# Where the products in front of a cross-attention are issued: into the tail of the mixture's blocks, on two fixed sets of banks

## The reference, cut to what matters

```python
x = x + _L0_xattn_ref(_layernorm(x), ctx_512, ctx_512)
x = x + _L0_ffn_ref(_layernorm(x), ...)        # 2 of 8 experts per token, then the weighted sum of two rows
x = x + _L1_xattn_ref(_layernorm(x), ctx_512, Wq, w_kc_q, w_kc_kv, W_qr, W_kr, Wo)   # 16 heads
x = x + _L1_ffn_ref(_layernorm(x), ...)        # 1 of 32 masked experts per token

q_hk  = (hidden_q @ Wq.T).reshape(Bv, Sv, H, K)
q_big = jnp.einsum('bshk,hkq->bshq', q_hk, w_kc_q)          # Wq and w_kc_q can be multiplied beforehand
q_r   = jnp.einsum('bshq,hqr->bhsr', rope(q_big), W_qr)
k_r   = jnp.einsum('bld,hdr->bhlr', kv_r, W_kr)
scores = jnp.einsum('bhsr,bhlr->bhsl', q_r, k_r)            # W_qr and W_kr likewise
ctx_lat = jnp.einsum('bhsd,hkd->bhsk', ctx_c, w_kc_kv)
return ctx @ Wo.T                                           # w_kc_kv and Wo likewise
```

## Time and profile before

| | us |
|---|---|
| median of 3 runs (range) | 478.03 (476.23 to 480.19) |
| profiled execution, its own time | 480.91 |
| its span, first to last instruction | 479.0 |
| busy in the span: PE / DVE / ACT / POOL | 379.1 / 347.0 / 213.7 / 137.9 |
| mean granted clock of TensorE | 0.919 of full speed |

### The profile page before, as it was taken

One profiled execution on the slowest core, in us unless ns is written; L12 is line 12 of the kernel. 1 busy time (PEld: TensorE's weight loads), 2 busy tenths in 40 slices (PEclk: granted clock), 3 DMA queues, 4 the chain that ended last, 5 costly groups with the idle time before them and its releaser, 6 DMA issues.

```text
span 479.0 us, 10598 instructions
## 1 busy us (share of the span) xinstructions
PE 379.1 (79%) x3676; PEld 259.6 (54%) x3677; DVE 347.0 (72%) x876; ACT 213.7 (45%) x474; POOL 137.9 (29%) x147
## 2 busy tenths in 40 slices
PE   2566867771687778797989999999999989548991
PEld 1344545671244444575555664664655878436881
DVE  4998898979788989386686876977868525663551
ACT  1578787825278778479010231221211321224440
POOL 1064000020667774300031421412403410161332
PEclk9989798955589999899999999999999999859997
DMA  8975562041144661171021120220220201341010
GB/s 299 423 300 189 191 219 104 10 168 46 39 132 152 196 200 57 46 263 36 1 90 47 42 90 9 82 89 2 89 89 1 89 1 54 124 130 58 25 35 22
DMA packets 16895, 50.77 MB, mean 106 GB/s; under 512 B 2072, under 2 KB 6304, under 8 KB 14800
## 3 DMA queue, kind: packets, MB, share of 16 engines
q1 hardware_dynamic: 13984, 42.46, 24.6%
q0 software_dynamic: 2864, 7.68, 5.3%
HBM read 43.44 MB, written 6.69 MB: 105 GB/s over the span
## 4 chain that ended last, share of the span: by engine, by line
PE 61%; DVE 14%; ACT 10%; issue 8%; POOL 5%; DMA 1%; ACTq 0%; DVEq 0%; POOLq 0%
PE bank L941 15%; PE bank L1147 7%; PE bank L953 6%; PE bank L1024 6%; PE bank L964 3%; PE bank L837 3%; PE bank L650 2%; PE bank L1000 2%; PE bank L977 2%; DVE mx L1426 2%; PE bank L803 2%; POOL y_rows L589 2%; ACT pnat L1166 2%; ACT W L1180 2%; POOL xg L582 1%
## 5 line engine op out<-in xcount | busy, mean ns | idle before, releaser
L1637 DVE TENSOR_TENSOR roped<-bank,cst 128x512 f32<-128x512 f32 x96 | 61.8, 686 | 30.2 <-PE bank L941 28.6
L596 POOL TENSOR_TENSOR WE<-WE,wT 128x512 f32<-128x512 f32 x32 | 40.5, 1299 | 140.9 <-DMA WE<-_L_ffn_expert_masks_dram 140.9
L1307 ACT ACTIVATE qrT<-bank 128x512 f32<-128x512 f32 x16 | 8.7, 596 | 82.2 <-PE bank L964 82.2
L941 PE MATMUL bank<-XNT_hi,AW_hi 128*128 128x512 f32 x96 | 41.3, 430 | 2.3 <-DVE roped L1637 1.6
L941 PE MATMUL bank<-XNT_hi,AW_lo 128*128 128x512 f32 x96 | 37.8, 394 | 0.0
L941 PE MATMUL bank<-XNT_lo,AW_hi 128*128 128x512 f32 x96 | 37.8, 393 | 0.0
L953 PE MATMUL bank<-roped,MW 128*64 128x512 f32 x128 | 31.0, 605 | 0.0
L1024 PE MATMUL bank<-VW,ctxT 128*128 128x256 f32 x128 | 30.8, 386 | 0.0
L941 PEld LDWEIGHTS bank<-XNT_hi,AW_hi 128*128 128x128 f32 x96 | 18.0, 187 | 22.0 <-DVE roped L1637 12.1
L582 POOL DMA_INDIRECT xg<-x_rows,owner_b x23 | 22.8, 993 | 24.0 <-DVE owner_b L420 14.8
L803 PE MATMUL bank<-W,xgT 128*128 x92 | 27.1, 422 | 2.2 <-ACT xgT L1243 2.2
(11 more groups left out here) (297 smaller groups left out, 893.9 us busy)
## 6 DMA issues: line engine op xcount, KB each, us to landing
raw<-in_L_ffn_w_dram SPq DMA_DIRECT2D x8, 1536.0 KB, 6.4
fold<-in_L_xattn_fold_dram SPq DMA_DIRECT2D x8, 1024.0 KB, 5.2
WE<-_L_ffn_expert_masks_dram SPq DMA_DIRECT2D x8, 1024.0 KB, 5.4
kv<-in_keys_values_dram SPq DMA_DIRECT2D x8, 656.0 KB, 7.6
yg<-y_rows SPq DMA_DIRECT2D x8, 256.0 KB, 4.7
x_tok<-pay SPq DMA_DIRECT2D x8, 256.0 KB, 2.3
X<-in_x_dram SPq DMA_DIRECT2D x4, 256.0 KB, 9.3
ctx_sb<-in_ctx_dram SPq DMA_DIRECT2D x1, 768.0 KB, 18.4
```

What stands on the lines that cost most here:

```text
L596: pool.tensor_tensor(WE[:, e], WE[:, e], wT[:], ALU.mult).then_inc(WE_ready, 1)
L941: mm = pe.matmul(bank[g][:], a[:, k, c * P:(c + 1) * P], b[:, k, g * 512:(g + 1) * 512], start=k == 0 and i == 0, stop=k == 1 and i == 2)
L1637: ins = dve.tensor_tensor(roped[n][:, r, :].rearrange("p (b s) -> p b s", s=S), src, cst[:, None, at:at + S].to_broadcast([P, 8, S]), ALU. ...
```

## The change

The fold of unit 0 is finished inside the tail: its query halves are issued one before and one after the turn of block 20, its values behind them, its keys after the turn of block 21; unit 1's query halves stand around the turn of block 22. ACT copies unit 0's rounded halves out between `hidT` and `y` of the last two blocks. Even units use banks 7, 0, 1, 3 and odd units 2, 4, 5, 6. Units 0, 1 and 2 (before: 0 and 1) are split by DVE straight from the bank. The variances are taken in two halves of four tiles, each half's inverse root is one power on POOL, and DVE centres all eight tiles. The rows are turned on banks 0, 1, 3, 7, and ACT copies them out before it evicts unit 7's values and keys, for which the first key product now waits too. SP's order does not change.

The diff, cut to its core:

```diff
-FOLD_BANKS = ((7, 0, 1, 3),) + 3 * ((4, 5, 6, 7), (0, 1, 2, 3)) + ((4, 5, 6, 7),)
+FOLD_BANKS = 4 * ((7, 0, 1, 3), (2, 4, 5, 6))
+TURN_BANKS = (0, 1, 3, 7)
+N_DIRECT = 3
 # GpSimd, behind the last store of y
+            link(pool.memset(minus_half[:], -0.5))
+            for h in range(2):
+                pool.wait_ge(var_ready, h + 1)
+                pool.tensor_tensor(rstd[:, 4 * h:4 * h + 4], var[:, 4 * h:4 * h + 4], minus_half[:, 4 * h:4 * h + 4], ALU.pow).then_inc(root_ready, 1)
...
 # TensorE
+            def fold_queries(u, c):
+                if c == 0:
+                    pe.wait_ge(unit_loaded[u], 32)
+                if u >= 2:
+                    pe.wait_ge(*query_evicted(u - 2, c))
...
+            for j in range(NBLK - 3, NBLK):
+                if j == NBLK - 3:
+                    fold_queries(0, 0)
+                elif j == NBLK - 1:
+                    pe.wait_ge(hid_done, NBLK + 2)
+                    fold_queries(1, 0)
+                turn_hidden(j % 4, j // 2)
+                if j == NBLK - 3:
+                    fold_queries(0, 1)
+                    pe.wait_ge(hid_done, NBLK + 1)
+                    fold_values(0)
+                elif j == NBLK - 2:
+                    fold_keys(0)
+                else:
+                    fold_queries(1, 1)
+                down(j, j % 2, in_run(word, j - 4 * ROUNDS))
...
+            fold_values(1)
             pe.wait_ge(y_copied, NBLK + 1)
-            fold_keys(0)
-            for u in range(1, NU):
-                fold_queries(u)
+            fold_keys(1)
+            for u in range(2, NU):
...
             for h in range(NT // 2):
-                if h == 0:
-                    pe.wait_ge(XN_ready, 2)
-                if h == NT // 4:
-                    pe.wait_ge(XN_acted, NT // 2)
+                pe.wait_ge(XN_ready, h + 2)
...
 # ScalarE
                 hidden_rows(j, j % 2)
+                if j >= NBLK - 2:
+                    high_part(0, j - NBLK + 2)
...
+                if u == NU - 1:
+                    for h in range(NT // 2):
+                        act.wait_ge(rows_turned, NT // 2 + h + 1)
+                        act.activation(XNT_hi[...], bank[TURN_BANKS[h]][...], ACT.Copy).then_inc(rowsT_ready, 1)
+                values_and_keys(u)
...
 # VectorE
+            def half_variances(h):
+                for t in range(4 * h, 4 * h + 4):
+                    ins = dve.bn_aggr(mv[:, t, :], stats[:, t, :])
+                link(ins)
+                dve.tensor_scalar(var[:, 4 * h:4 * h + 4], mv[:, 4 * h:4 * h + 4, 1], EPS, None, ALU.add).then_inc(var_ready, 1)
...
-            aggregate()
+                if t == NT // 2 - 1:
+                    half_variances(0)
+            half_variances(1)
             dve.wait_ge(M_ready, 4)
-            for t in range(NT // 2):
+            for h in range(2):
+                dve.wait_ge(root_ready, h + 1)
+                for t in range(4 * h, 4 * h + 4):
+                    centred_rows(t)
...
-                if u + 2 < NU:
+                if N_DIRECT <= u + 2 < NU:
                     split_rest(u + 2)
```

More of the change, by code:

```diff
@@ L823, in down, with query_evicted @@
                 mm.then_inc(y_ready, 1)
-            def fold_queries(u):
-                pe.wait_ge(unit_loaded[u], 32)
-                for c in range(2):
-                    at = bank[FOLD_BANKS[u][c]]
-                    if u == 2:
-                        pe.wait_ge(*((A_split, 2), (M_done, 1))[c])
-                    elif u == 3:
-                        pe.wait_ge(A_split, 3 + c)
-                    elif u > 3:
-                        pe.wait_ge(A_copied, 2 * (u - 4) + c + 1)
-                    for h in range(2):
-                        mm = pe.matmul(at[:, h * QD:(h + 1) * QD], f_wq[u][:, h, c * P:(c + 1) * P],
-                                       f_kcq[u][:, h, :], start=True, stop=True)
-                    mm.then_inc(A_ready, 1)
+            def query_evicted(u, c):
+                return (A_split, 2 * u + c + 1) if u < N_DIRECT else (A_copied, 2 * (u - N_DIRECT) + c + 1)
@@ new lines, in first_keys_evicted, with keys_evicted @@
+            def first_keys_evicted(u):
+                return (M_done, u + 1) if u < N_DIRECT else (M_copied, 2 * (u - N_DIRECT) + 1)
+            def keys_evicted(u):
+                return (M_done, u + 1) if u < N_DIRECT else (M_copied, 2 * (u - N_DIRECT) + 2)
+            def fold_queries(u, c):
[4 more added lines that the diff above has]
+                for h in range(2):
+                    mm = pe.matmul(bank[FOLD_BANKS[u][c]][:, h * QD:(h + 1) * QD], f_wq[u][:, h, c * P:(c + 1) * P],
+                                   f_kcq[u][:, h, :], start=True, stop=True)
+                mm.then_inc(A_ready, 1)
@@ L885, in _ @@
             word = run_of(ROUNDS)
-            for k in range(RUN):
+            for k in range(RUN - 3):
                 j = 4 * ROUNDS + k
@@ L945, in to_keys_outer @@
             def to_keys_outer(u, g):
+                if u == g == 0:
+                    pe.wait_ge(*query_evicted(NU - 1, 1))
+                    pe.wait_ge(V_done, NU)
+                    pe.wait_ge(*keys_evicted(NU - 1))
                 if g == 0:
-                    pe.wait_ge(*keys_folded(u))
+                    pe.wait_ge(*keys_evicted(u))
                     pe.wait_ge(qrT_ready, 2 * u + 2)
@@ L1265, in scale_hidden, with high_part @@
                 act.activation(hid[j % 4][:], hid[j % 4][:], ACT.Identity, scale=hs[j % 4][:, 4:5], bias=magic[:]).then_inc(hid_acted, 1)
+            def high_part(u, c):
+                act.wait_ge(A_ready, 2 * u + c + 1)
+                act.activation(AW_hi[u][:, c, :], bank[FOLD_BANKS[u][c]][:, 0:2 * QD], ACT.Copy).then_inc(A_done, 1)
             for j in range(4):
@@ L1283, in _, with values_and_keys @@
             act.sem_inc(ctxT_ready, 2)
-            def fold(u):
+            def values_and_keys(u):
                 banks = [bank[i] for i in FOLD_BANKS[u]]
-                for c in range(2):
-                    act.wait_ge(A_ready, 2 * u + c + 1)
-                    act.activation(AW_hi[u][:, c, :], banks[c][:, 0:2 * QD], ACT.Copy).then_inc(A_done, 1)
-                if u >= 2:
+                if u >= N_DIRECT:
                     for c in range(2):
@@ L1318, in contexts @@
                     act.activation(ctxT[:, u, g * 512:(g + 1) * 512], bank[6 + g][:], ACT.Copy).then_inc(ctxT_ready, 1)
-            for u in range(NU):
+            values_and_keys(0)
+            for u in range(1, NU):
                 if u == NU - 2:
@@ L1323, in _ @@
                         act.wait_ge(y_stored[r], 16 * len(range(r, NBLK, 4)))
[L1324 to L1331 removed]
+                for c in range(2):
+                    high_part(u, c)
+                if u == NU - 1:
+                    for h in range(NT // 2):
+                        act.wait_ge(rows_turned, NT // 2 + h + 1)
+                        act.activation(XNT_hi[:, :, 2 * h * P:2 * (h + 1) * P], bank[TURN_BANKS[h]][:].rearrange("p (k n) -> p k n", k=2),
+                                       ACT.Copy).then_inc(rowsT_ready, 1)
+                values_and_keys(u)
             for u in range(NU):
@@ L1653, in by_sum, with centred_rows, add_experts @@
                 dve.tensor_tensor(prob[:, :, h, :], prob[:, :, h, :], s_stat[:, h, 2, :, None].to_broadcast([P, NT, S]), ALU.mult).then_inc(prob_ready, 1)
-            fold(0)
-            fold(1)
-            for t in range(NT):
+            def centred_rows(t):
+                ins = dve.tensor_scalar(XN[:, t, :], X[:, t, :], mv[:, t, 0:1], rstd[:, t:t + 1], ALU.subtract, ALU.mult)
+                if t % 2:
+                    ins.then_inc(XN_ready, 1)
+            def add_experts(t):
                 dve.wait_ge(rows_in[t // 2], 48)
```

68 lines of the change are left out of this document (24 added, 44 removed).

## The result

The changed kernel took **476.00 us** (median of 20 runs, 471.76 to 480.31) beside 479.74 for the kernel before in the same set (20 runs, 475.53 to 483.64). The ratio is 0.9914, with a 95% interval of 0.9889 to 0.9939: a gain of 0.86%, or 4.1 us, between 2.9 and 5.3. The ratio is of the runs within 1.5% of their kernel's fastest, so that it differs a little from the quotient of the two medians (0.9922). The profiled execution took 474.75, its span is 472.8.

A forecast was written before the change was run, and what follows sets the result against it. It took PE's folds and ACT behind them to bound the join, with DVE's path next; 4.5 + 0.55 = 5.0 us off gave a median of 473.0 us, own range 471.0 to 474.5, full range 470.6 to 476.6.

The forecast's parts named there:

- line at 1%: About 1% (4.8 us, at 473.25) can be told from no change; chances: faster 0.45, same 0.49, slower 0.06.
- the sum: Whole kernel: 4.5 us earlier at the first projection plus 0.55 in the loop, 5.0 us saved.
- the roots: Join: POOL powers of 1.04 each, both hidden; rival (13%): first stops an addition 1.04 or second sticks out 1.2, 474.1.
- PE's rivals: Join: PE's folds or its clock stay on the path, each costing 1.35 or more; 474.4 to 476, 17%.
- The tail: Last blocks: moved products and copies mostly fit PE's and ACT's waits; last `y` 0.3 us earlier.
- the third direct unit: Folds: DVE is through unit 2 by 204.1, or 205.5 if the clock falls, still covered before the additions.
- The start of DVE's path: Join: first addition set by the rows' landing, not the folds; 205.6 in place of 205.93.
- DVE's path: Join: additions 12.03, aggregates 1.12, centring 2.74, subtractions 1.30; first projection at 222.8, 4.5 us earlier.
- TensorE's slack: Join: PE waits 0.85 for unit 7's weights, ends at 218.5, 0.9 us before the first centred pair.
- The loop: First trip: unit 2's `split_rest` leaves the stretch where PE waited 1.62 for DVE; 0.55 us saved, bounds 0 and 0.95.

The follow-up runs named there:

- the tail undone: Changed kernel with unit 0's key products and copies and unit 1's query products put back behind the last block; median 476.2 us, ratio 0.9884.
- the second profile: The changed kernel run again as it is, nothing altered; median 475.46 us (6 runs), ratio 0.99.
- the root put back: Changed kernel with one aggregation of all eight tiles and the inverse root on DVE, without halves and POOL roots; median 478.41 us, ratio 0.9985.
- the pairs: Changed kernel with DVE's additions and statistics of two tiles interleaved, same instructions otherwise; median 473.32 us, ratio 0.9846.
- the doubled root: Changed kernel with the second POOL root computed twice before DVE is told; run once, 476.93 us.
- the late load: Changed kernel with the third 1 MB mask load issued only after unit 1's contexts; median 475.41 us, ratio 0.9906.
- the last run: Changed kernel with paired additions, early fold 7 load, late third mask load, and the last two centred tiles on POOL; median 472.80 us, ratio 0.9864.

## Why the prediction was right, and where it was not

It said 473.0 with a range of 470.6 to 476.6, and 476.00 came out, in the range and 3.0 above the forecast. By the forecast's own line at 1% that is no change that could be told, to which it had given 0.49; with 20 runs of each the interval is half a per cent wide, and the gain is clear. Of the 3.0, 1.7 are the kernel before, which had a median of 479.74 in this set and not 478.03. The other 1.3 are the saving: 3.7 between the medians where the sum was 5.0. That 476.00 lies in the range is partly luck: it is outside the forecast's own 471.0 to 474.5, in the part that was added for the roots and for PE's rivals, and neither of them came. Counted from 479.74, its own range would end at 476.2.

*The tail* was right: 0.40 for the 0.3 taken. So was the third direct unit, taken to end at 204.1: it ended at 201.15, 13.76 behind the common point, for 13.7. That it is in time only with the products moved into the tail is what the tail undone adds.

*The start of DVE's path*: 0.35 earlier for 0.33, bound by the rows as foreseen, with 1.42 of waiting. *DVE's path*: 17.38 from the first addition to the projection, and 17.13 in the second profile, for 17.2; the first has a wait of 0.30 for the third tile's rows in it. So the projection came 4.32 and 4.60 earlier for 4.5. That this path sets the end is shown from both sides: the root put back costs 2.2 to 2.4, the pairs win 1.5 to 1.8, and 1.4 us more for TensorE costs at most 0.4.

*The roots.* The first cost nothing: the additions at 209.35 and 209.86 ran beside the power of 209.59 in 0.48 each, 0.52 apart, as elsewhere. They have two inputs in SBUF, so by the rule of the Trainium skill that the prediction weighed (SBUF — State Buffer, Who interferes with whom) one of them should have been shut out for most of 1.15 us; the trace disagrees here too. The second was only just covered. It took 1.26 and not 1.04, ended 0.04 before the fifth centred tile, and put 0.1 on the eight tiles (2.85 for 2.74). This term was mis-sized by 0.2, and the cover of 1.37 was almost used up, as the doubled root showed.

*TensorE's slack* was mis-sized: 2.0 and 1.7 for 0.9. The wait of 0.85 for fold 7 did not come. Among the DMA issues of the change (last number us to landing) it has

```profile
fold<-in_L_xattn_fold_dram SPq DMA_DIRECT2D x1, 1024.0 KB, 8.4
```

where the forecast took the 9.4 of before; issued at 203.05 it was there at 211.45, just ahead of unit 7 at 211.78. In the run with the pairs alone, where TensorE did wait for it, it was 0.78. A slack that is too large was counted as harmless, but it is a wait of TensorE. Behind waits of 1.7 to 2.0 the clock stayed at 1.00 in two profiles and fell in two (the doubled root, the late load); behind 2.65 and 4.00 it fell. A fall cost 0.2 to 1.0 between the first projection and the keys product, and more in the turns.

*The loop*: 0.58 and 0.56 for 0.55, and the wait of 1.07 as forecast.

*What failed* is the sum's silence on the rest of the loop: a saving was taken as kept to the end. The stop in unit 1's contexts took back 1.40 in one profile and 1.18 in the other. With it the terms make 4.32 + 0.58 - 1.40 = 3.5 and 4.60 + 0.56 - 1.18 = 4.0 at the end of the loop, beside 3.7 to 4.1 between the runs. The two profiles themselves don't keep this to the end: from the common point they gain 3.1 and 2.1, since behind the loop they take 0.4 and 1.9 more than the kernel before, where the other profiles take from 0.2 less to 0.5 more. Of the terms, the bank sets and the order of ACT's copies were not undone by themselves.

## What to carry to other kernels

When products leave a stretch that another engine bounds next, the gain is what that engine's path loses: cost the second path first, step by step, and make the first engine only as early as it needs to be, because its new wait may bring its clock down. A saving ahead of a long loop is not safe until the loop's transfers are looked at: a large load that meets an instruction transfer can take a microsecond back, and moving that load by a few microseconds is a cheap trial. And steps in which each instruction reads what the last one wrote can gain from being interleaved two by two, here a quarter of their time.

## What the runs showed of the hardware

- An instruction transfer that met a 1 MB load at about 400 GB/s landed 47.0 to 47.5 us behind the first keys product and TensorE stood 0.9 to 1.2 us; with the load moved it landed at 45.0 to 45.5 and TensorE did not stand. TensorE went on 1.3 to 1.5 us after the end of the transfer's packet in all nine stops. Eight more instructions on TensorE moved a stop of 1.4 to 1.6 to unit 4.
- Two tiles' additions and statistics on DVE took 3.00 one after the other and 2.25 interleaved, by the order and the waits that go with it.
- Centred tiles of 128x256 took GpSimd 0.60 each early in the kernel and 1.21 and 1.37 behind its root in the last run, with DVE at work beside it both times. Why they differ was not tried.
- Behind waits of TensorE of 1.72 and 1.99 us the granted clock stayed at 1.00, behind waits of 1.85 and 1.97 it fell to 0.50, one profile each. What decides it stays open.
